# Weight quotients moved from VectorE to GpSimd in a cross-attention and block-quantised MLP kernel

## The chip, the cores and the metric

One core of a Trainium2 chip. The metric is device time of one launch in microseconds; less is better. PE is TensorE, DVE VectorE, ACT ScalarE, POOL (or Pool) GpSimd, SP SyncE, which here only issues DMAs.

## The reference

There are four batches (B = 4) of x [512, 512] and of a context [512, 256].

```python
x = x + x_att(layernorm(x), ctx)          # query = ctx Wq' + bq, key = ctx Wk' + bk
                                          # x_m = l . softmax(query key')'
x = x + ffn(layernorm(x))
# ffn: v = bf16(x); h = bf16(layernorm(v) * w + b)
#      h = bf16(mx(h) mx(W1)' + b1); h = bf16(gelu_tanh(h))
#      h = bf16(mx(h) mx(W2)' + b2); out = bf16(v + h)
def mx_quant(x):                          # blocks of 32 along the contraction axis
    amax = max(abs(block))
    scale = exp2(floor(log2(amax)) - 6)
    return clip(round(x / scale), -128, 127) * scale
```

W1 is [2048, 512] and W2 [512, 2048], both float32, and both are quantised on the chip in every launch.

## The kernel before, in words

Each engine has a program of its own, written out by hand in one order, and waits on semaphores; engines work strictly in that order. Batches are pipelined: while PE multiplies the attention of batch b, DVE and ACT prepare the softmax of batch b + 1 (its "front"), and ACT and Pool work on the second layernorm of batch b - 1.

**DVE** (from L760). `front(b, ...)` (L969) has, for each of four row tiles t, `negmax` (minus the row maxima of the energies in PSUM), `normalise` (x - mean, times the factor rx), `recip` and `recip_scaled` (one over the row sum, from ACT's exp), `p_low` and `x_low` (the low float16 halves of P and x). Between them stand the steps of the weights. A unit of weights is [128, 2048] float32; there are four of W1 and four of W2 (u = 0 to 3), and a unit takes seven steps, counted by `w_step`: `w_amax` (L791, largest of each block of 32), `w_power`, `w_scale`, `w_inverse` (tiny: power of two, scale and its inverse), `w_over` (L804, weight times inverse to int16), `w_clip` (L810), `w_mult` (L814, int16 times scale to bfloat16). `back(b, ...)` (L1032) holds `w_amax` of W2, the last `p_low`, the tail of an earlier batch (`times_w` and `plus_b` for four tiles: the layernorm's weight and bias into `hq`) and W1's clip and mult. `x_stats(b)` (L914) has four bn_stats and four bn_aggr of x for the next batch. `h1_*` is the same block quantisation for `hq`. The calls stand from L1057 on. After the batches come the slots (L1080), which quantise the gelu's output, 128 rows at a time.

**Pool** (from L335) has tiny operations on [128, 4]: `factors_x(b)` (from bn_aggr's output to `rx`; `normalise(b, 0)` waits for it), `mean_x1`, `factors_x1(b)` (scale and offset of the first normalisation of v; ACT's `v_out(b)` waits for `off`), `factors_v(b)` (from ACT's sums of v; `times_w(b, 0)` waits for it). Their order is set by `batch` and the calls from L410 on. In the MLP, Pool adds the residual, two operations of [128, 512] per tile.

**ACT** (from L436): `batch(b, front, qk, v)` (L511) has a loop over t with `exp`, `x_high`, `p_high`, `x_plus` (attention output of batch b from PSUM), `load_w1`/`load_w2` (DMA of the next unit, as soon as the one before has been read), `v_sums`, `v_out`, `context`; then `query_key` for the batch after and four `x1_square`. After the batches (L574 on): `v_out(2, .)`, `v_sums(2, .)`, then `x_plus(3, 0)`, `y_out(0, 0)`, and so on.

**PE** (from L610): `values(b, t)` (L652) waits for all four transposed tiles of P; `energies`, `queries_keys`. Its order in a batch (L667) is context, then `energies(front, t + 2)` and `values(b, t)` in turn, then the queries, keys and first two energies of the next. From L727: `values(3, 0)`, `product1(0, 0)`, `values(3, 1)`, `product1(0, 1)`, `values(3, 2)`, `values(3, 3)`, `product1(1, 0)`, and the steps of the MLP. `product1(m, k)` waits until `y_out` has read the PSUM banks of the tile before.

**SP** (from L214) issues the DMA transposes in order: four of x, four of P, then w2 of the unit before and w1 of this one, in each front (L231).

Of the kernel before, what the change touches and what calls it, by code (L numbers as in the profile page):

```python
# [15 lines left out]
P = 128  # L16
# [8 lines left out]
W_STEPS = 7  # L25
# [4 lines left out]
def xattn_ffn_kernel(nc, x, ctx_in, wq, bq, wk, bk, ln_w, ln_b, w1, b1, w2, b2, out):  # L30
# [25 lines left out]
    with ExitStack() as stack:  # L56
# [3 lines left out]
        def sem(name):  # L60
            return stack.enter_context(nc.semaphore(name))
# [106 lines left out]
        nm, off_rdy = sem("nm"), sem("off_rdy")  # L168
        v_mean, v_mean2, v_ms = sem("v_mean"), sem("v_mean2"), sem("v_ms")
# [166 lines left out]
        def _(pool):  # L336
# [49 lines left out]

            factors_x(0)
# [13 lines left out]
            def batch(b, x, v):  # L401

                if x is not None:
                    factors_x(x)
                if v is not None:
                    factors_v(v)
                mean_x1(b)
                factors_x1(b)
# [28 lines left out]
        def _(act):  # L437
# [73 lines left out]
            def batch(b, front, qk, v):  # L511

                for t in range(LT + 1):
                    if t < NT:
                        exp(front, t)
                        x_high(front, t)
                    if t > 0:
                        p_high(front, t - 1)  # L520
                    if b is not None and t > 1:
                        x_plus(b, t - 2)
                    if t == 2 and b is not None:
                        load_w2(front)
# [6 lines left out]
                if not isinstance(front, int) or front + 1 < B:  # L531
                    load_w1(front + 1)
# [229 lines left out]
        def _(dve):  # L762
# [41 lines left out]
            def w_over(a, u):  # L804
                dve.wait_ge(w_step[a], W_STEPS * u + 4)
                inverse = mxi[:, a, :, 0:1].broadcast_to([P, NB, BLOCK])
                dve.tensor_tensor(blocks(w_int[:, :]), blocks(wst[:, a, :]), inverse, ALU.mult)\  # L807
                   .then_inc(w_step[a], 1)

            def w_clip(a, u):  # L810
                dve.wait_ge(w_step[a], W_STEPS * u + 5)
                dve.tensor_scalar(w_int[:, :], w_int[:, :], QMAX, None, ALU.min).then_inc(w_step[a], 1)

            def w_mult(a, u):  # L814
                wait(dve, (w1T_rdy, w2T_rdy)[a], 16 * u)
                dve.wait_ge(w_step[a], W_STEPS * u + 6)
                dve.tensor_tensor(pairs(wquant[:, a, :]), pairs(w_int[:, :]), per_block(mxs[:, a, :, :]), ALU.mult)\
                   .then_inc(w_step[a], 1)
# [95 lines left out]
            def x_stats(b):  # L914
                if isinstance(b, int):
                    dve.wait_ge(ld_x[b], 16)
                for t in range(LT):
                    dve.bn_stats(stats[:, t, :], xs[:, LT * b + t, :]).then_inc(st, 1)  # L918
                if isinstance(b, int) and b > 0:
                    dve.wait_ge(rx_rdy, b)  # L920
                for t in range(LT):
# [47 lines left out]
            def front(b, w1, w2, stats_next, h1):  # L969

                negmax(b, 0)
                normalise(b, 0)
                if w1 is not None:
                    w_amax(W1, w1)

                negmax(b, 1)
                normalise(b, 1)  # L980
                recip(b, 0)
                if w1 is not None:
                    w_power(W1, w1)
                recip_scaled(b, 0)
                if w1 is not None:
                    w_scale(W1, w1)
                x_low(b, 0)
                if w1 is not None:
                    w_inverse(W1, w1)
                if h1 is not None:  # L990
                    h1_amax(h1)

                negmax(b, 2)
                normalise(b, 2)
                recip(b, 1)
                if h1 is not None:
                    h1_power(h1)
                recip_scaled(b, 1)
                p_low(b, 0)
                if h1 is not None:  # L1000
                    h1_scale(h1)
                x_low(b, 1)
                if h1 is not None:
                    h1_inverse(h1)
                if w2 is not None:
                    w_over(W2, w2)

                negmax(b, 3)
                normalise(b, 3)
                recip(b, 2)  # L1010
                if h1 is not None:
                    h1_over(h1)
# [3 lines left out]
                if h1 is not None:  # L1016
                    h1_clip(h1)
                if w2 is not None:
                    w_clip(W2, w2)
                    w_mult(W2, w2)  # L1020

                recip(b, 3)
                p_low(b, 2)
                recip_scaled(b, 3)
                x_low(b, 3)
                w_over(W1, b)
                if stats_next is not None:
                    x_stats(stats_next)
                if h1 is not None:
                    h1_mult(h1)  # L1030

            def back(b, w1, w2, tail):  # L1032


                w_amax(W2, w2)
                p_low(b, NT - 1)
                w_power(W2, w2)
                if tail is not None:
                    times_w(tail, 0)
                w_scale(W2, w2)  # L1040
                if tail is not None:
                    plus_b(tail, 0)
                w_inverse(W2, w2)
                if tail is not None:
                    for t in range(1, LT):
                        times_w(tail, t)
                        plus_b(tail, t)
                w_clip(W1, w1)
                w_mult(W1, w1)
# [15 lines left out]
            x_stats(0)  # L1065
            front(0, None, None, 1, None)
            back(0, 0, 0, None)
            front(1, 1, 0, 2, None)
            back(1, 1, 1, None)
            dve.wait_ge(ld_ln, 32)  # L1070
            front(2, 2, 1, 3, None)
            back(2, 2, 2, 0)
            for b in range(3, B):
                front(b, b, b - 1, None, b - 3)
                back(b, b, b, b - 2)
            for part in tail_parts(B - 3)[LT:]:
                for part_step in part:
                    part_step()
# [26 lines left out]
            w_over(W2, B - 1)  # L1105
# [50 lines left out]
```

## Time and profile before

| | us |
|---|---|
| median of 3 runs | 284.21 |
| lowest, highest | 283.39, 287.79 |
| profiled execution, its own time | 283.25 |
| its span in the profile | 281.4 |

| engine | busy us | share of the span |
|---|---|---|
| PE | 228.7 | 81% |
| DVE | 249.2 | 89% |
| ACT | 169.4 | 60% |
| POOL | 69.0 | 25% |

Times in the rows are microseconds from the start of the span. A timeline row has start, duration, engine, line, operation, output and input, and in brackets the idle time ahead of it and what ended that. In grouped rows the numbers behind the shapes are the count, the busy time with the mean of one in ns, and the idle time ahead of them. Consecutive instructions overlap by some 0.1 us, so that the distance of two starts is a little less than the duration. PEclk is TensorE's granted clock as a share of full speed.

### The profile page before, as it was taken

What the parts mean: (1) busy time and instruction counts of PE and PEld (TensorE: products, weight loads), DVE (VectorE), ACT (ScalarE), POOL (GpSimd) and SP (SyncE); (2) the same over time, 40 slices, a digit from 0 to 9 for tenths busy, and PEclk for the clock granted to TensorE, in tenths of its full rate; (3) what the DMA queues carried; (4) which work ended last, traced back from release to release, by engine and by line L of the source; (5) the groups of instructions that cost most, each with busy time, mean ns of one, the idle gap of its engine ahead of it and who ended that gap; (6) DMA issues with size and microseconds to landing.
All of it is one profiled execution on the core that took longest, in us unless ns stands there. A gap on an engine that the chain in (4) does not pass through costs nothing.

```text
span 281.4 us, 3244 instructions
## 1 busy us (share of the span) xinstructions
PE 228.7 (81%) x937; PEld 99.4 (35%) x946; DVE 249.2 (89%) x377; ACT 169.4 (60%) x287; POOL 69.0 (25%) x96
## 2 busy tenths in 40 slices
PE   7748739996998059651699969799999989999993
PEld 7314313443433024210244433344444434444431
DVE  2388999999988899999979999599999999877992
ACT  2337216628995447845987599966566554665610
POOL 1058100022004500053060050413333233333400
PEclk9985886999999759975899999999999999999999
DMA  4963999999997952939623045635355555555683
GB/s 157 378 250 89 227 279 201 297 238 194 263 257 190 221 91 38 222 59 194 124 52 62 0 93 70 119 62 123 88 122 129 130 130 131 130 130 114 139 178 130
DMA packets 103077, 42.92 MB, mean 152 GB/s; under 512 B 93844, under 2 KB 96152, under 8 KB 102552
## 3 DMA queue, kind: packets, MB, share of 16 engines
q1 hardware_dynamic: 100224, 35.93, 58.6%
q10 hardware_dynamic: 2360, 6.83, 7.7%
q8 instruction: 5, 0.08, 0.1%
q0 software_dynamic: 480, 0.02, 0.1%
q14 instruction: 8, 0.07, 0.1%
HBM read 15.48 MB, written 4.19 MB: 70 GB/s over the span
## 4 chain that ended last, share of the span: by engine, by line
DVE 45%; PE 25%; ACT 11%; DMA 8%; issue 5%; POOL 4%; SPq 2%; ACTq 0%; DVEq 0%; POOLq 0%
DVE amax L764 12%; PE ps L722 9%; PE ps L712 8%; PE ps L661 4%; DVE w_int L807 4%; DMA xhl<-pf 3%; DVE hq L966 3%; DVE stats L918 3%; DMA wst<-in_L_ffn_W 3%; DVE vw L961 3%; DVE pf L871 3%; DVE phl L942 2%; DVE wquant L861 2%; POOL rs L350 2%; DVE xhl L954 2%
## 5 line engine op out<-in xcount | busy, mean ns | idle before, releaser
L661 PE MATMUL ps<-pT,xT 128*128 128x512 f16 x192 | 49.7, 414 | 14.1 <-DMA pT<-phl 11.0
L722 PE MATMUL ps<-w2T,xhl 128*128 128x512 bf16 x247 | 56.5, 379 | 2.9 <-DMA xhl<-pf 2.4
L712 PE MATMUL ps<-w1T,cxT 128*128 128x512 bf16 x256 | 58.0, 380 | 0.0
L558 ACT ACTIVATE wst<-ps 128x1024 bf16<-128x1024 f32 x32 | 32.3, 1019 | 27.9 <-PE ps L712 27.9
L764 DVE TENSOR_REDUCE amax<-phl 128x64 f32<-128x2048 bf16 x16 | 36.5, 2280 | 6.9 <-ACT phl L562 6.9
L649 PE MATMUL ps<-qkT 128*128 128x512 f32 x32 | 19.5, 715 | 22.7 <-ACT pf L457 18.8
L661 PEld LDWEIGHTS ps<-pT,xT 128*128 128x128 f16 x192 | 19.9, 106 | 48.0 <-issue 31.8
L722 PEld LDWEIGHTS ps<-w2T,xhl 128*128 128x128 bf16 x256 | 24.6, 98 | 33.2 <-DMA xhl<-pf 4.2
L712 PEld LDWEIGHTS ps<-w1T,cxT 128*128 128x128 bf16 x256 | 23.7, 98 | 32.6 <-issue 6.2
L562 ACT ACTIVATE phl<-wst 128x2048 bf16<-128x2048 bf16 x16 | 30.6, 1910 | 1.3
L423 POOL TENSOR_TENSOR wst<-wst,vs 128x512 bf16<-128x512 bf16 x12 | 14.8, 1233 | 55.5 <-DVE wquant L866 55.5
L764 DVE TENSOR_REDUCE amax<-wst 128x64 f32<-128x2048 f32 x8 | 18.2, 2270 | 6.1 <-DMA wst<-in_L_ffn_W 6.1
L457 ACT ACTIVATE pf<-ps,nmax 128x512 f32<-128x512 f32 x16 | 10.9, 681 | 19.8 <-DVE nmax L928 19.7
L571 ACT ACTIVATE wst<-ps 128x512 bf16<-128x512 f32 x16 | 9.5, 595 | 16.2 <-PE ps L722 15.8
L861 DVE TENSOR_TENSOR wquant<-phl,mxi 128x2048 int16<-128x2048 bf16 x15 | 18.3, 1223 | 0.3
L641 PE MATMUL ps<-cxT,wqkT 128*128 128x512 f32 x32 | 16.5, 663 | 2.5 <-ACT cxT L447 2.5
L807 DVE TENSOR_TENSOR w_int<-wst,mxi 128x2048 int16<-128x2048 f32 x8 | 18.3, 2285 | 0.0
L871 DVE TENSOR_TENSOR pf<-wquant,mxs 128x2048 bf16<-128x2048 int16 x15 | 18.2, 1216 | 0.0
L649 PEld LDWEIGHTS ps<-qkT 128*128 128x128 f32 x32 | 5.9, 212 | 32.3 <-ACT pf L457 21.8
L355 POOL TENSOR_SCALAR rs<-mv 128x4 f32<-128x4 f32 x4 | 0.9, 227 | 65.6 <-DVE mv L923 65.6
L664 PE MATMUL ps<-xs,ident_x 128*128 128x512 f32 x32 | 16.3, 592 | 0.0
L482 ACT ACTIVATE xs<-ps 128x512 f32<-128x512 f32 x16 | 9.4, 586 | 9.7 <-PE ps L664 9.7
(79 smaller groups left out, 357.4 us busy)
## 6 DMA issues: line engine op xcount, KB each, us to landing
wst<-in_L_ffn_W ACTq DMA_DIRECT2D x6, 1024.0 KB, 6.1
xs<-in_x SPq DMA_DIRECT2D x4, 1024.0 KB, 8.4
out_x<-wst SPq DMA_DIRECT2D x16, 256.0 KB, 2.8
cx<-in_ctx SPq DMA_DIRECT2D x4, 512.0 KB, 5.8
wst<-in_L_ffn_W SPq DMA_DIRECT2D x2, 1024.0 KB, 10.3
xhl<-pf SPq DMA_TRANSPOSE x17, 4.3
xT<-xhl SPq DMA_TRANSPOSE x16, 4.6
pT<-phl SPq DMA_TRANSPOSE x16, 3.3
```

Of the source, the lines that this page charges most:

```text
L558: act.activation(ys[:, k, 1024 * g:1024 * g + 1024], ps_y[:, 2 * g:2 * g + 2, :], ACT.Copy)\
L562: act.activation(gs[:, k, :], ys[:, k, :], ACT.Gelu_apprx_tanh).then_inc(g_rdy, 1)
L641: last = pe.matmul(ps_qk[:, a, :], wqkT[:, a, c, :], cxT[:, c, :], start=(c == 0), stop=(c == CT - 1))
L649: pe.matmul(ps_e[:, t % 2, :], qkT[:, 0, P * t:P * t + P], qkT[:, 1, :], start=True, stop=True).then_inc(e_ps, 1)
L661: pe.matmul(ps_pv[:, t % 2, :], xT[:, t, NT * a + n, :], pT[:, :, NT * c + n, :], start=(s == 0), stop=False)
L664: pe.matmul(ps_pv[:, t % 2, :], ident_x[:, :], xs[:, LT * b + t, :], start=False, stop=True).then_inc(pv_ps, 1)
L712: last = pe.matmul(ps_y[:, c, :], h1T[:, k, t, :], w1T[:, 4 * c:4 * c + 4, t, :], start=False, stop=(t == KT - 1))
L722: last = pe.matmul(ps_z[:, k, :], h2T[:, k, t, :], w2T[:, t, :], start=False, stop=(t == FT - 1))
L764: dve.tensor_reduce(amax[:, a, :], by_block, AX_X, ALU.max, apply_absolute_value=True)\
L807: dve.tensor_tensor(blocks(w_int[:, :]), blocks(wst[:, a, :]), inverse, ALU.mult)\
L861: dve.tensor_tensor(pairs(h2u[:, k, :]), pairs(gs[:, k, :]), per_block(mxi[:, k, :, :]), ALU.mult).then_inc(h2_step[k], 1)
L871: dve.tensor_tensor(pairs(h2q[:, k, :]), pairs(h2u[:, k, :]), per_block(mxs[:, k, :, :]), ALU.mult).then_inc(h2_step[k], 1)
```

## The change

The quotient of each weight unit, `w_over` on DVE, becomes `over_scale` on Pool: in place in `wst`, in float32, counted by new semaphores `w_u`. `w_clip` on DVE reads `wst` and converts to int16, so a unit has six steps in place of seven. Pool's order is written out, with four waits (`p_lo` or `h_rdy`) ahead of W2's quotients. DVE's `front` has a new fixed order and takes in what `back` held. A unit of W2 gets its maxima in its own front and its clip and mult in the next. The tail of a batch stands between fronts, and `h1_*` behind `front(3)`, except `h1_amax(0)`. ACT's loop has one step more, and v's sums and outputs are one step later in it. In the diff, helpers and steps that only change place are left out.

```diff
-W_STEPS = 7
+W_STEPS = 6
...
+            def over_scale(a, u):
+                pool.wait_ge(w_step[a], W_STEPS * u + 4)
+                w = blocks(wst[:, a, :])
+                inverse = mxi[:, a, :, 0:1].broadcast_to([P, NB, BLOCK])
+                pool.tensor_tensor(w, w, inverse, ALU.mult).then_inc(w_u[a], 1)
+
+            over_scale(W1, 0)
             factors_x(0)
...
             factors_x(1)
-            batch(0, 2, None)
-            for b in range(1, B - 2):
-                batch(b, b + 2, b - 1)
-            batch(B - 2, None, B - 3)
-            factors_v(B - 2)
-            mean_x1(B - 1)
-            factors_x1(B - 1)
-            factors_v(B - 1)
+            pool.wait_ge(p_lo, NT)
+            over_scale(W2, 0)
+            over_scale(W1, 1)
+            factors_x(2)
+            mean_x1(0)
+            pool.wait_ge(p_lo, 2 * NT)
+            over_scale(W2, 1)
+            factors_x1(0)
+            over_scale(W1, 2)
+            factors_x(3)
+            factors_v(0)
+            mean_x1(1)
+            pool.wait_ge(h_rdy, LT)
+            over_scale(W2, 2)
+            factors_x1(1)
+            over_scale(W1, 3)
+            factors_v(1)
+            mean_x1(2)
+            pool.wait_ge(h_rdy, 2 * LT)
+            over_scale(W2, 3)
+            factors_x1(2)
+            factors_v(2)
+            mean_x1(3)
+            factors_x1(3)
+            factors_v(3)
...
-                for t in range(LT + 1):
+                for t in range(LT + 2):
                     if t < NT:
                         exp(front, t)
                         x_high(front, t)
-                    if t > 0:
+                    if 0 < t <= NT:
                         p_high(front, t - 1)
-                    if b is not None and t > 1:
+                    if b is not None and 1 < t < LT + 1:
                         x_plus(b, t - 2)
-                    if t == 2 and b is not None:
+                    if t == 1 and b is not None:
                         load_w2(front)
-                    if v is not None and t > 0:
-                        v_sums(v, t - 1)
-                    if v is not None and t < LT:
-                        v_out(v, t)
+                    if t == LT and front + 1 < B:
+                        load_w1(front + 1)
+                    if v is not None and t > 1:
+                        v_sums(v, t - 2)
+                    if v is not None and 0 < t <= LT:
+                        v_out(v, t - 1)
...
             def w_clip(a, u):
-                dve.wait_ge(w_step[a], W_STEPS * u + 5)
-                dve.tensor_scalar(w_int[:, :], w_int[:, :], QMAX, None, ALU.min).then_inc(w_step[a], 1)
+                wait(dve, w_step[1 - a], W_STEPS * (u + a))
+                dve.wait_ge(w_u[a], u + 1)
+                dve.tensor_scalar(w_int[:, :], wst[:, a, :], QMAX, None, ALU.min).then_inc(w_step[a], 1)
```

The new order of `front(b)` on DVE, in full ("later" is b > 0; `x_moments` and `x_aggregate` are the two halves of `x_stats`):

```python
negmax(b, 0)
w_amax(W1, b)                      # later
negmax(b, 1); normalise(b, 0); normalise(b, 1)
w_clip(W2, b - 1)                  # later
recip(b, 0); w_power(W1, b)        # later
recip_scaled(b, 0); w_scale(W1, b) # later
x_low(b, 0); w_inverse(W1, b)      # later
negmax(b, 2)
x_moments(b + 1)                   # b = 3: h1_amax(0)
recip(b, 1); normalise(b, 2); recip_scaled(b, 1); p_low(b, 0)
w_mult(W2, b - 1)                  # later
x_low(b, 1)
negmax(b, 3); w_clip(W1, b); recip(b, 2); normalise(b, 3)
recip_scaled(b, 2); p_low(b, 1); x_low(b, 2); w_mult(W1, b)
recip(b, 3); w_amax(W2, b); recip_scaled(b, 3); p_low(b, 2)
w_power(W2, b); x_low(b, 3); w_scale(W2, b)
x_aggregate(b + 1)                 # b < 3
w_inverse(W2, b); p_low(b, 3)
```

The calls: `x_moments(0)`, `x_aggregate(0)`, `front(0)`, `front(1)`, `front(2)`, `tail(0)`, `front(3)`, `h1_power` to `h1_mult` of batch 0, `tail(1)`, all six `h1_` steps of batch 1, then `w_clip(W2, 3)` and `w_mult(W2, 3)`, and from there as before. In W1's case `w_power` to `w_inverse` of unit 0 stand ahead of `x_moments(0)`, as before of `x_stats(0)`.

## Rows read from the trace of the kernel before

**Rows 1.** Windows: length, then busy PE, PEld, DVE, ACT, POOL; PEclk, DMA, GB/s.

```profile
39.00:65.60 26.60, 23.61 (x72) 9.82 (x73) 26.12 (x48) 14.37 (x32) 1.71 (x4) 0.87 1.11 248
65.60:100.10 34.50, 22.84 (x82) 9.75 (x79) 31.54 (x55) 24.41 (x59) 8.32 (x15) 0.92 0.97 215
100.10:134.40 34.30, 21.14 (x65) 8.46 (x66) 33.98 (x55) 22.89 (x55) 6.32 (x9) 0.75 0.62 124
```

**Rows 2.** Grouped instructions of 0 to 160 us: DVE's whole-unit and 512-wide operations.

```profile
L807 DVE TENSOR_TENSOR w_int<-wst,mxi 128x2048 int16<-128x2048 f32 x8 | 18.3, 2285 | 0.0
L764 DVE TENSOR_REDUCE amax<-wst 128x64 f32<-128x2048 f32 x8 | 18.2, 2270 | 6.1 <-DMA wst<-in_L_ffn_W 6.1
...
L928 DVE TENSOR_REDUCE nmax<-ps 128x1 f32<-128x512 f32 x16 | 10.9, 681 | 0.2 <-PE ps L649 0.2
...
L918 DVE BATCH_NORM_STATS2 stats<-xs 128x6 f32<-128x512 f32 x16 | 9.9, 680 | 0.0
...
L949 DVE TENSOR_SCALAR xn<-xs,mv,rx 128x512 f32<-128x512 f32 x16 | 8.6, 537 | 1.3 <-POOL rx L358 1.3
...
L812 DVE TENSOR_SCALAR w_int<-w_int 128x2048 int16<-128x2048 int16 x8 | 5.5, 687 | 0.0
```

**Rows 3.** The chain that ended last: first normalise, and the seam to batch 1.

```profile
18.90 0.56 DVE xn L949
...
36.69 3.09 SPq L244
39.83 3.21 DMA pT<-phl
```

**Rows 4.** Timeline of PE: values, queries and keys, first product.

```profile
43.28 4.51 PE L661 MATMUL ps<-pT,xT 128*128 128x512 f16 x12 [0.60 <-DMA pT<-phl]
...
59.69 3.60 PE L641 MATMUL ps<-cxT,wqkT 128*128 128x512 f32 x8
...
147.13 0.40 PE L707 MATMUL ps<-b1row,ones 3*128 3x512 bf16 x4
```

**Rows 5.** Timeline of all engines, 122 to 146 us.

```profile
124.76 5.36 SPq L244 DMA_TRANSPOSE pT<-phl  x4
...
131.79 0.75 DVE L966 SCALAR_TENSOR_TENSOR hq<-vw,rs,lnb 128x512 bf16<-128x512 f32 x1
...
132.64 2.93 ACT L497 ACTIVATE vs<-xs,off,rs 128x512 bf16<-128x512 f32 x4 [3.00 <-POOL off L370]
...
140.94 0.58 ACT L482 ACTIVATE xs<-ps 128x512 f32<-128x512 f32 x1
...
143.79 1.02 ACT L558 ACTIVATE wst<-ps 128x1024 bf16<-128x1024 f32 x1 [0.70 <-PE ps L712]
```

**Rows 6.** Timeline of POOL.

```profile
66.91 0.20 POOL L366 TENSOR_SCALAR rs<-sums 128x4 f32<-128x4 f32 x1 [4.53 <-ACT vs L490]
...
68.31 0.20 POOL L370 TENSOR_TENSOR off<-mean,rs 128x4 f32<-128x4 f32 x1
...
129.72 0.64 POOL L366 TENSOR_SCALAR rs<-sums 128x4 f32<-128x4 f32 x1 [3.04 <-ACT vs L490]
...
132.07 0.53 POOL L370 TENSOR_TENSOR off<-mean,rs 128x4 f32<-128x4 f32 x1
...
179.18 0.23 POOL L376 TENSOR_SCALAR mean<-sums 128x4 f32<-128x4 f32 x1 [12.82 <-ACT vs L508]
...
180.73 1.04 POOL L350 TENSOR_TENSOR rs<-rs,half 128x4 f32<-128x4 f32 x1
...
191.40 1.15 POOL L429 TENSOR_TENSOR wst<-xs,wst 128x512 f32<-128x512 f32 x1
```

**Rows 7.** Timeline of DVE: w_inverse and the power step of two units.

```profile
14.16 0.20 DVE L783 TENSOR_SCALAR mxi<-mxs 128x128 uint16<-128x128 uint16 x1
...
185.14 0.20 DVE L772 TENSOR_SCALAR pow<-amax 128x64 uint32<-128x64 uint32 x1
...
192.25 0.35 DVE L772 TENSOR_SCALAR pow<-amax 128x64 uint32<-128x64 uint32 x1
```

More of the change, by code:

```diff
@@ L912, in split3, with x_moments, x_aggregate @@
                 dve.tensor_copy(part[:, 2, :], f[:, 0, :]).then_inc(step, 1)
[L914 to L916 removed]
+            def x_moments(b):
+                dve.wait_ge(ld_x[b], 16)
                 for t in range(LT):
                     dve.bn_stats(stats[:, t, :], xs[:, LT * b + t, :]).then_inc(st, 1)
[L919 removed]
+            def x_aggregate(b):
+                if b > 0:
                     dve.wait_ge(rx_rdy, b)
+                    dve.wait_ge(xn_rdy, LT * b)
                 for t in range(LT):
@@ L967, in plus_b, with front @@
                                          ALU.mult, ALU.add).then_inc(h_rdy, 1)
-            def front(b, w1, w2, stats_next, h1):
+            def front(b):
+                later = b > 0
                 negmax(b, 0)
+                if later:
+                    w_amax(W1, b)
+                negmax(b, 1)
                 normalise(b, 0)
-                if w1 is not None:
-                    w_amax(W1, w1)
-                negmax(b, 1)
                 normalise(b, 1)
+                if later:
+                    w_clip(W2, b - 1)
                 recip(b, 0)
-                if w1 is not None:
-                    w_power(W1, w1)
+                if later:
+                    w_power(W1, b)
                 recip_scaled(b, 0)
-                if w1 is not None:
-                    w_scale(W1, w1)
+                if later:
+                    w_scale(W1, b)
                 x_low(b, 0)
[L988 to L991, printed above, removed]
+                if later:
+                    w_inverse(W1, b)
                 negmax(b, 2)
+                if b + 1 < B:
+                    x_moments(b + 1)
+                else:
+                    h1_amax(b - 3)
+                recip(b, 1)
                 normalise(b, 2)
-                recip(b, 1)
-                if h1 is not None:
-                    h1_power(h1)
                 recip_scaled(b, 1)
                 p_low(b, 0)
-                if h1 is not None:
-                    h1_scale(h1)
+                if later:
+                    w_mult(W2, b - 1)
                 x_low(b, 1)
[L1003 to L1006, printed above, removed]
                 negmax(b, 3)
+                w_clip(W1, b)
+                recip(b, 2)
                 normalise(b, 3)
-                recip(b, 2)
-                if h1 is not None:
-                    h1_over(h1)
                 recip_scaled(b, 2)
@@ L1015, in front, with tail @@
                 x_low(b, 2)
[L1016 to L1020, printed above, removed]
+                w_mult(W1, b)
                 recip(b, 3)
+                w_amax(W2, b)
+                recip_scaled(b, 3)
                 p_low(b, 2)
-                recip_scaled(b, 3)
+                w_power(W2, b)
                 x_low(b, 3)
[L1026 to L1049, printed above, removed]
+                w_scale(W2, b)
+                if b + 1 < B:
+                    x_aggregate(b + 1)
+                w_inverse(W2, b)
+                p_low(b, 3)
+            def tail(b):
+                for t in range(LT):
+                    times_w(b, t)
+                    plus_b(b, t)
             def tail_parts(b):
@@ L1064, in _ @@
             w_inverse(W1, 0)
[L1065 to L1069, printed above, removed]
-            dve.wait_ge(ld_ln, 32)
[L1071 to L1078, printed above, removed]
+            x_moments(0)
+            x_aggregate(0)
+            front(0)
+            front(1)
+            dve.wait_ge(ld_ln, 32)
+            front(2)
+            tail(0)
+            front(3)
+            h1_power(0)
+            h1_scale(0)
+            h1_inverse(0)
+            h1_over(0)
+            h1_clip(0)
+            h1_mult(0)
+            tail(1)
+            h1_amax(1)
+            h1_power(1)
+            h1_scale(1)
+            h1_inverse(1)
+            h1_over(1)
+            h1_clip(1)
+            h1_mult(1)
             def slot(m, k, tail, first=False, last=False):
```

18 lines of the change are left out of this document (2 added, 16 removed).

## Prediction, made before the changed kernel was run

> **What bounds the kernel now.** I read the busy table by stretches first, then the grouped instructions, then the chain that ended last, and last the timelines of the four engines around the seams between batches. The stretches [rows 1] are cut where DVE begins `front(1)` to `front(3)`: 39.0, 65.6 and 100.1 us. DVE is busy 26.1 of 26.6 us in batch 1, 31.5 of 34.5 in batch 2 and 34.0 of 34.3 in batch 3, so it looks like the bound, and eight `w_over` of 2.285 us are its dearest removable piece [rows 2]. But PE is busy 23.6 of 26.6 us in batch 1, and ACT 24.4 of 34.5 us in batch 2. So I looked at who stands just behind DVE.
>
> Seam 1 to 2: the last transposed P of batch 0 lands at 43.0 us [rows 3], PE begins `values(0,0)` at 43.3 and `queries_keys(2)` at 59.7 [rows 4], and DVE's `negmax(2,0)`, which needs the energies made from them, starts at 65.6 [rows 1]. DVE was just about on time: PE's path from landed P to the next energies is 65.6 - 43.3 = 22.3 us long.
>
> Seam to the MLP: `plus_b(1,3)` is over at 132.5, the offset `off` of batch 2 at 132.6, and ACT starts `v_out(2,.)` at 132.6, then the v sums, and reaches `x_plus(3,0)` at 140.9, the first half of `y_out(0,0)` behind it [rows 5]. PE begins `product1(0,1)` at 147.1 [rows 4]; it wants both halves of `y_out(0,0)`.
>
> **What is removed and added on DVE.** Eight `w_over` go: seven inside the batches, each holding the next instruction back by 2.2 us, one after them. `w_clip` now reads float32, not int16. Its price lies between 0.69 us (the int16 clip, L812) and 2.15 us (four times the 512-wide float32 tensor_scalar of L949, 0.537 us, start cost and all) [rows 2]. I take 1.4, nearer to L949 with the start cost paid once, 0.7 more than now. So batch 1, once 26.5 us of solid DVE work, would be 26.5 - 2 x 2.2 + 2 x 0.7 = 23.5; I use 22.5 to 23.5 for one `front`.
>
> **The quotient on Pool.** No Pool operation of 2048 columns is in the trace. Four times the 512-wide two-input one is 4.6 us [rows 6]; with start cost taken out (L370, 128x4, 0.2 us) it is 0.2 + 4 x 0.95 = 4.0. I take 4.3. A broadcast operand in blocks of 32 could make it dearer; 2.3 us (DVE's own time for it) and 9 us (double the 512 row's rate) are the far ends.
> The Trainium skill ("GPSIMD Engine Reference", section "Elementwise — side-by-side cycle accounting") has Pool's float32 tensor_tensor of 2048 at 4497 ns against 2293 on DVE; the trace agrees for DVE (2285 ns), and no row has the other. By it each quotient would be 0.2 us longer than I take.
>
> **Its gates.** A Pool operation under way holds DVE up. At 192.25 DVE's `power` takes 0.35 us while a Pool addition that ends at 192.55 is running; at 185.14, with Pool idle, it takes 0.20 [rows 6, 7]. The reductions that stand beside such additions keep their 2.28 us, like those without (the `w_amax`, 2.27 us [rows 2]).
> The Trainium skill ("SBUF — State Buffer", section "Who interferes with whom") says the same as a lock held for the whole instruction, against DVE operations in a two-port mode or with two SBUF inputs.
> So each quotient has a window. W2's: `negmax`, `w_amax`, `negmax` = 0.6 + 2.2 + 0.6 = 3.4 us, then `normalise`. W1's: `negmax` and four bn_stats = 0.6 + 2.4 = 3.0 us, then `normalise` [rows 2]. A quotient of 4.3 us leaves DVE waiting 4.3 - 3.4 = 0.9 us and 4.3 + 0.1 - 3.0 = 1.4 us: per batch 2.3 us of the 2 x (2.2 - 0.7) = 3.0 us saved are given back. From both sides the wait is 0 (no blocking) to 5 us each (9 us quotient).
>
> **Front(0).** `over_scale(W1,0)` is queued on Pool ahead of `factors_x(0)`. The first `normalise`, at 18.9 us [rows 3], needs that. The quotient starts near 14.4 us (as `w_inverse` ends [rows 7], beside the bn_stats) and ends near 18.7, and factors_x takes 1.7: normalise starts at 20.5, 1.6 us late. DVE then saves its 2.2 and pays 0.7. ACT comes to `query_key(1)` only after `p_high(0,3)`, which the new order has later. I get front(1) at 38.1, not 39.0.
> `p_low(0,3)` is now last in the front, at 37.2 (before 36.0, released at 36.7 [rows 3]), and, more important, `x_low(0,3)` is near 36 and SP transposes in order: xT 3, pT 0, 1, 2, 3. At a free queue four take 5.36 us [rows 5], 1.3 each: pT 3 is issued at 36.0 + 4 x 1.3 = 41.2 and lands 3.2 later, at 44.4. Beside a weight load one waits 3.09 us for its turn [rows 3]; with two such steps it is 48. W1(1) is loaded from 35.4 in the new order, so I take 45.0 against 43.0.
>
> **Batch 1 and 2.** PE's path is the later one: front(2) = 45.0 + 22.3 - 0.3 = 67.0 (DVE alone would be there at 38.1 + 23.2 + 1.4 = 62.7 and waits 4.3 us). That is 1.4 us later than before, although DVE does less. In front(2) ACT's v sums are one step later in its loop than before: `p_high(2,3)` is released by `recip_scaled(2,3)`, some 19.8 us into the front (22.5 less three 512-wide operations and small ones), plus 1.4 of lock. Then `p_high` 0.6, `x_plus` 0.7, load 0.4, v_sums 1.4, v_out 0.7, v_sums 1.4 (eight steps of v_out and v_sums took 140.9 - 132.6 = 8.3 us [rows 5]): 26.4. Pool's `factors_v` takes 2.6 (179.18 to 181.77 [rows 6]) and tail(0) 6.0, as before. Front(3) = 67.0 + 26.4 + 2.6 + 6.0 = 102.0, before 100.1.
>
> **Front(3) and what follows.** Here both locks count (W2's is let go by tail(0) itself): v sums end at 102.0 + 25.0 + 2.3 = 129.3; factors_v 131.9; tail(1), behind `h1_mult(0)`, which is over by then, ends at 137.9. Before, it ended at 132.5 [rows 5].
> Now the term that decides. Pool waits for `h_rdy` = 8 (the end of tail(1)), does `over_scale(W2,3)`, 4.3 us, and only then `factors_x1(2)`, 1.6 us alone (66.91 to 68.51) or 2.9 beside DVE's work (129.72 to 132.60) [rows 6]; I take 2.3. `off` is there at 137.9 + 4.3 + 2.3 + 0.2 = 144.7, before at 132.6. ACT is in order, so v_out(2), v_sums(2), `x_plus(3,0)` and `y_out(0,0)` all move by 12.1 us. PE had slack there: `y_out(0,0)` could have let product1(0,1) go at 140.94 + 0.7 + 2 x 1.0 = 143.6 and it started at 147.1 [rows 4, 5], because values(3,1) was in between, which is now done early: 3.5 us. Net 12.1 - 3.5 = +8.6.
> What is won beside that isn't waited for: product1(0,0) waits for the transposed W1(3), no longer a matter of the last DVE operation of the batch, and could start at 136, not 139.8; the last `w_over`, 140.6 to 142.8, has nobody waiting. From `product1(0,1)` on, nothing is changed, and PE, ACT and DVE keep their order, so the 8.6 us arrive at the end.
>
> **The sum.** The profiled execution took 283.25 us (span 281.4); 283.25 + 8.6 = 291.9. The median of the runs is 1.0 above it: 284.2 + 8.6 = 292.8.
> Ends. Low: no blocking (front(3) and tail(1) 2.3 + 1.4 earlier), landing at 44.4 (0.6), quotient 4.0 and factors 1.6 (1.0), tail stretches half a us shorter each: 8.6 - 6.3 = +2.3, so 286.5. High: landing at 48 (3.0), quotient 4.6 with its waits (1.2), factors 2.9 (0.6), and PE idle for over 10 us before product1(0,1), which in stretches where it idles so has a granted clock of 0.75 to 0.87 [rows 1], 1 us: +14, 298.
>
> **Rivals.**
> A, faster: the queues of ACT and Pool follow DVE instead of limiting it. For it: DVE's 91 to 99% in the three stretches [rows 1]. Seven times 2.2 - 0.7 = 10.5 us saved in the first stage; the part that can pass the join is the 4 us of product1(0,0) at least: 273.7 to 280, say 278. It needs `off(2)` before 136 us, and I find tail(1) alone ending later than that; against it also PE's 22.3 us path.
> B, within 2%: the same chain, with Pool and DVE not blocking each other and the transposes prompt: 286.5. For it: nothing in the trace shows a float32 DVE operation of 512 columns blocked.
> C, slower still: the broadcast quotient costs some 9 us. Then +4.7 directly at W2(3) and 4.7 in each of three locks and in front(0) that pass through: 284.2 + 8.6 + 4.7 + 10 = 307. Nothing for it but that no row shows such an operation.
> D, the change doesn't do what it says: a quotient stands beside reductions only for its first 3 us. That is part of my forecast.
>
> **How the numbers follow.** Forecast (288.5 to 297) 0.62, B 0.20, A 0.12, C 0.06. The likeliest is 292.8. The range, 285.5 to 298.5, takes in B and leaves out A and C and little more. Some 2% (5.7 us, above 289.9 or under 278.5) is what a measurement of this kernel can tell from no change: 0.58 of the forecast's 0.62 and C are over it; its other 0.04, B and 0.02 of A within. Slower 0.64, same 0.26, faster 0.10.
>
> **What would show it.** Right: Pool TENSOR_TENSOR of 128x2048 near 4.3 us; `normalise` lengthened right behind reductions; DVE idle some 4 us before `negmax(2,0)` and before tail(0); a Pool quotient between the last `plus_b` of tail(1) and `factors_x1(2)`, v_out(2) starting near 145; PE idle before product1(0,1) near 155. Wrong: front(3) starting before 95 us, or v_out(2) before 136; a span without those PE gaps.

## The result, and the profile after

The changed kernel takes 306.06 us (303.44 to 306.54, 4 runs) against 283.8 us: a ratio of 1.079, 95% interval 1.070 to 1.089. It is slower, as forecast, but by 22.3 us where 8.6 were forecast, and lies outside the range. A few executions of a kernel are over 1.5% slower than its fastest; medians here include them, ratios and intervals leave them out. The profiled execution took 306.54 us with a span of 304.7 us, 23.3 more than before.

The windows of the changed kernel, columns as in [rows 1], cut where DVE begins `front(1)`, `front(2)` and `front(3)`, where tail(1) ends, and at 205 us:

```profile
36.40:75.60 39.20, 24.20 (x81) 10.46 (x80) 22.32 (x44) 14.06 (x31) 13.25 (x9) 0.83 0.90 204
75.60:117.50 41.90, 25.10 (x82) 10.22 (x80) 27.98 (x52) 25.15 (x61) 9.87 (x14) 0.85 0.98 178
117.50:152.20 34.70, 21.10 (x69) 8.44 (x70) 32.11 (x52) 21.46 (x52) 12.37 (x11) 0.80 0.66 138
152.20:205.00 52.80, 42.73 (x190) 17.43 (x189) 42.61 (x51) 41.57 (x73) 12.03 (x19) 0.93 0.33 60
```

Front(1) begins at 36.4 us, 2.6 us earlier than before. Then batch 1 takes 39.2 us (before 26.6) and batch 2 takes 41.9 us (before 34.5), and DVE is busy for only 22.3 and 28.0 us of them, where it was busy for 26.1 and 31.5 [rows 1]. Batch 3 takes 34.7 us (before 34.3). So front(3) is 17.4 us late (117.5 against 100.1), and the other 23.3 - 17.4 = 5.9 us come after it.

What DVE and PE waited for, from their timelines (start us, us, instruction, idle before and releaser). DVE:

```profile
38.80 2.29 DVE L781 TENSOR_REDUCE amax<-wst 128x64 f32<-128x2048 f32 x1 [1.73 <-DMA wst<-in_L_ffn_W]
...
41.60 0.99 DVE L962 TENSOR_SCALAR xn<-xs,mv,rx 128x512 f32<-128x512 f32 x2
...
55.87 2.47 DVE L929 BATCH_NORM_STATS2 stats<-xs 128x6 f32<-128x512 f32 x4 [10.41 <-DMA xs<-in_x]
...
75.61 0.69 DVE L941 TENSOR_REDUCE nmax<-ps 128x1 f32<-128x512 f32 x1 [4.75 <-PE ps L666]
...
95.54 1.23 DVE L829 TENSOR_TENSOR wquant<-w_int,mxs 128x2048 bf16<-128x2048 int16 x1 [7.75 <-DMA w2T<-wquant]
```

PE:

```profile
53.28 4.82 PE L678 MATMUL ps<-pT,xT 128*128 128x512 f16 x12 [14.22 <-DMA pT<-phl]
...
168.76 0.61 PE L724 MATMUL ps<-b1row,ones 3*128 3x512 bf16 x4 [6.77 <-ACT wst L575]
169.31 5.71 PE L729 MATMUL ps<-w1T,cxT 128*128 128x512 bf16 x16
```

The three longest of these waits were not there before: DVE stands 10.41 us for the load of x(2), 7.75 us in `w_mult(W2,1)` for w2T(0), and PE 14.22 us for pT(0,3), which comes at 53.0 (before 43.0 [rows 3], when PE waited 0.60 us for it [rows 4]). All three are waits for DMAs. The timeline of the queues' issues shows what they ran beside. First ACT's issue of W2's load in batch 1, after and then before the change:

```profile
44.03 0.33 ACTq L494 DMA_DIRECT2D wst<-in_L_ffn_W  x1
```

```profile
49.38 0.33 ACTq L477 DMA_DIRECT2D wst<-in_L_ffn_W  x1
```

Then the issues of SP and ACT around w2T(0), in batch 2:

```profile
78.20 0.58 SPq L226 DMA_DIRECT2D xs<-in_x  x1
...
78.82 4.97 SPq L261 DMA_TRANSPOSE w2T<-wquant  x1
...
81.44 0.34 ACTq L494 DMA_DIRECT2D wst<-in_L_ffn_W  x1
...
83.84 11.37 SPq L255 DMA_TRANSPOSE w1T<-wquant  x1
```

And the chain of waits has how long the two transposes took to land:

```profile
43.72 9.32 DMA pT<-phl
...
53.28 4.82 PE ps L678 x12
...
75.61 0.69 DVE nmax L941
...
78.82 16.69 DMA w2T<-wquant
...
117.53 0.69 DVE nmax L941
...
152.28 3.64 POOL wst L393
...
157.82 2.93 ACT vs L514 x4
...
168.76 0.61 PE ps L724 x4
```

W2's load is issued at 44.03, right behind the transpose of pT(0,3) of 43.72, which then lands 9.32 us after its issue (before 3.2). In the kernel before that load was issued at 49.4. At 81.44 the next one goes out 2.6 us behind w2T(0), which takes 16.69 us. The last three rows are the join as forecast: tail(1) has ended, the quotient of W2(3) runs on Pool (152.28), the factors follow, ACT starts `v_out(2,.)` at 157.82 and PE `product1(0,1)` at 168.76. The wait of 6.77 us ahead of that has a second price. From 168.76 to 174.85 us TensorE's granted clock was 0.61, nearer to the lower of its two levels (half of full speed), and `product1(0,1)` took 6.1 us to the next `values`; before, after no such wait, the clock was 1.00 in that stretch and it took 3.8.

Pool's timeline, the first quotient and the join:

```profile
14.04 3.64 POOL L393 TENSOR_TENSOR wst<-wst,mxi 128x2048 f32<-128x2048 f32 x1 [11.78 <-DVE mxi L800]
...
152.28 3.64 POOL L393 TENSOR_TENSOR wst<-wst,mxi 128x2048 f32<-128x2048 f32 x1 [5.80 <-DVE hq L979]
156.01 0.28 POOL L367 TENSOR_SCALAR rs<-sums 128x4 f32<-128x4 f32 x1
156.37 1.04 POOL L351 TENSOR_TENSOR rs<-rs,half 128x4 f32<-128x4 f32 x1
157.49 0.30 POOL L371 TENSOR_TENSOR off<-mean,rs 128x4 f32<-128x4 f32 x1
```

The grouped instructions of 0 to 160 us:

```profile
L393 POOL TENSOR_TENSOR wst<-wst,mxi 128x2048 f32<-128x2048 f32 x8 | 29.1, 3641 | 31.7 <-DVE mxi L800 20.1 <-DVE hq L979 11.6
...
L824 DVE TENSOR_SCALAR w_int<-wst 128x2048 int16<-128x2048 f32 x8 | 9.7, 1216 | 0.0
...
L962 DVE TENSOR_SCALAR xn<-xs,mv,rx 128x512 f32<-128x512 f32 x16 | 9.1, 588 | 1.8 <-POOL rx L359 1.8
```

The quotient takes 3.64 us each time, the clip from float32 1.22 us, and `normalise` 0.59 us in the mean over sixteen (0.53 undisturbed): with the gates, the blocking that was priced at 2.3 us per batch is some 2 us in all (16 `normalise` 0.06 us longer each, and one `power` step, at 154.55, of 1.42 us where 0.19 is usual). In batches 1 and 2 DVE waited for x (10.41 and 1.23 us) while W1's quotient ran, so nothing was blocked there.

### The profile page after: what moved, and what is told of

Same layout as the page of the kernel before. It is cut to its first block, busy times and chain, and to the rows that moved or that the text cites. A ratio compares the mean times of both kernels' runs of the same rounds, so it can differ in the third digit from the quotient of the medians.

```text
span 304.7 us, 3264 instructions
## 1 busy us (share of the span) xinstructions
PE 231.5 (76%) x946; PEld 99.8 (33%) x946; DVE 237.6 (78%) x369; ACT 169.7 (56%) x287; POOL 92.6 (30%) x104
## 4 chain that ended last, share of the span: by engine, by line
DVE 32%; PE 25%; DMA 14%; ACT 13%; POOL 6%; issue 5%; SPq 4%; POOLq 0%; ACTq 0%; DVEq 0%
DVE amax L781 9%; PE ps L739 8%; PE ps L729 7%; PE ps L678 6%; DMA w2T<-wquant 5%; POOL wst L393 4%; DMA pT<-phl 3%; DMA xhl<-pf 3%; DVE vw L974 3%; DVE hq L979 3%; DMA wst<-in_L_ffn_W 3%; ACT squares L522 3%; SPq L245 2%; DVE pf L883 2%; ACT vs L514 2%
## 5 line engine op out<-in xcount | busy, mean ns | idle before, releaser
L678 PE MATMUL ps<-pT,xT 128*128 128x512 f16 x192 | 50.7, 420 | 37.4 <-DMA pT<-phl 25.8
L729 PE MATMUL ps<-w1T,cxT 128*128 128x512 bf16 x256 | 60.1, 389 | 0.0
L739 PE MATMUL ps<-w2T,xhl 128*128 128x512 bf16 x256 | 57.9, 379 | 1.2 <-DMA xhl<-pf 1.2
L393 POOL TENSOR_TENSOR wst<-wst,mxi 128x2048 f32<-128x2048 f32 x8 | 29.1, 3641 | 31.7 <-DVE mxi L800 20.1
L666 PE MATMUL ps<-qkT 128*128 128x512 f32 x32 | 18.5, 684 | 15.4 <-ACT pf L474 10.3
L486 ACT ACTIVATE xhl<-xn 128x512 f16<-128x512 f32 x16 | 10.0, 627 | 33.9 <-DVE xn L962 33.9
L974 DVE SCALAR_TENSOR_TENSOR vw<-vs,mean,lnw 128x512 f32<-128x512 bf16 x16 | 11.9, 746 | 13.4 <-POOL rs L351 13.4
L929 DVE BATCH_NORM_STATS2 stats<-xs 128x6 f32<-128x512 f32 x16 | 9.9, 680 | 11.6 <-DMA xs<-in_x 11.6
L873 DVE TENSOR_TENSOR wquant<-phl,mxi 128x2048 int16<-128x2048 bf16 x15 | 18.3, 1223 | 0.3
L883 DVE TENSOR_TENSOR pf<-wquant,mxs 128x2048 bf16<-128x2048 int16 x15 | 18.3, 1218 | 0.1
L356 POOL TENSOR_SCALAR rs<-mv 128x4 f32<-128x4 f32 x4 | 2.4, 608 | 48.6 <-DVE mv L937 48.5
```

The costliest lines, as they stand in the source:

```text
L393: pool.tensor_tensor(w, w, inverse, ALU.mult).then_inc(w_u[a], 1)
L666: pe.matmul(ps_e[:, t % 2, :], qkT[:, 0, P * t:P * t + P], qkT[:, 1, :], start=True, stop=True).then_inc(e_ps, 1)
L678: pe.matmul(ps_pv[:, t % 2, :], xT[:, t, NT * a + n, :], pT[:, :, NT * c + n, :], start=(s == 0), stop=False)
L729: last = pe.matmul(ps_y[:, c, :], h1T[:, k, t, :], w1T[:, 4 * c:4 * c + 4, t, :], start=False, stop=(t == KT - 1))
L739: last = pe.matmul(ps_z[:, k, :], h2T[:, k, t, :], w2T[:, t, :], start=False, stop=(t == FT - 1))
L873: dve.tensor_tensor(pairs(h2u[:, k, :]), pairs(gs[:, k, :]), per_block(mxi[:, k, :, :]), ALU.mult).then_inc(h2_step[k], 1)
```

## The experiments

The kernel before took 283.38 us beside the first four kernels that stand here (its repetition apart), 283.47 beside the three edits together and those built on them, 283.98 beside the two with the quotients on DVE, and 284.06 beside the repetition and the pair of two edits. All ratios are to these.

**The loads of x(2) and x(3) at once.**
```diff
             load_x(1)
+            load_x(2)
+            load_x(3)
...
-            front(0, None, 2)
-            front(1, 3, 3)
+            front(0, None, None)
+            front(1, 3, None)
```


> SP issues the loads of x(2) and x(3) at the start instead of behind the transposes of P. Theory A (the statistics of the next x, moved up in the front, stand before their data has landed): the idle 10.4 us ahead of x_moments(2) and 1.2 ahead of x_moments(3) go, and the time falls by about 10 us, to 296. Theory B (the weight load of W2, now issued one loop step earlier on ACT, shares the DMA engines with the transposes and delays them): the idle time only moves to negmax(1,3), because PE's values(0,0) still waits for transposed P until about 50 us; the time falls by 1 to 3 us, to 303 to 305, and the 7.7 us ahead of w_mult(W2,1) stay.

298.41 us (296.78 to 299.15), ratio 1.055 [1.051, 1.060], 7.7 us below the changed kernel. The wait for x(2) is gone, but pT(0,3) still lands 9.0 us after its issue and PE stands 13.7 us for it; DVE now waits 8.19 us for PE's energies instead, and front(2) starts at 75.1, where it did. So the 10.41 us for x(2) had hidden behind PE. What is won is w2T(0): with x(3)'s load out of its way it lands 4.5 us after its issue, DVE doesn't wait for it, and front(3) starts at 108.4. Neither theory held in full: A was right on the waits for x but had 10 us, B was right on PE but had the wait for w2T(0) stay.

**W2's load one step later.**
```diff
-                    if t == 1 and b is not None:
+                    if t == 2 and b is not None:
                         load_w2(front)
```


> ACT issues load_w2 at t == 2 again, not t == 1; nothing else. Theory A: no change beyond 1 us, since x(2) is issued where it was. Theory B: P(0,3) lands within 3 to 4 us of its issue, as before the change (near 47, not 53 us), w2T(0) lands within 8 us of its issue, not 16.7, so that the 7.7 us ahead of w_mult(W2,1) go; the time falls by 7 us or more, to 299 or less.

293.93 us (293.22 to 294.27), ratio 1.039 [1.034, 1.044], 12.1 us below the changed kernel. The load is issued at 54.6, behind the transposes; pT(0,3) lands 3.3 us after its issue, as theory B had it, PE begins `values(0,0)` at 47.2 instead of 53.3, w2T(0) takes 7.2 us (7.8 before the change) and nobody waits for it, and even the wait for x(2) is halved (5.45 us). Front(2) starts at 70.2, front(3) at 104.8. The load beside the transposes is thus the larger part of the two.

**The factors ahead of the quotient at the join.**
```diff
             mean_x1(2)
+            factors_x1(2)
             pool.wait_ge(h_rdy, 2 * LT)
             over_scale(W2, 3)
-            factors_x1(2)
```


> On Pool factors_x1(2) stands ahead of the gate h_rdy = 8 and of over_scale(W2,3), not behind them. Theory C (the step named in the prediction: ACT's v_out(2) and all behind it wait for off(2), which stands in Pool's queue behind tail(1) and a quotient): off(2) is there near 151, not 157.8 us, product1(0,1) starts near 162 and not at 168.8, and the time falls by 6 to 7 us, to 299.5. Rival: DVE or PE would be as late anyway, and the time stays within 1 us of 306.

293.51 us in the middle of 290.29, 291.79, 295.24 and 302.84; they are too far apart for an interval. In the profile `off(2)` is done at 144.7 with the quotient behind it, and PE's wait before `product1(0,1)` falls from 6.77 to 0.74 us. From front(3) to the end of the span it takes 290.0 - 110.0 = 180.0 us, where the changed kernel takes 304.7 - 117.5 = 187.2. That is the expected 7 us; but front(3) itself began at 110.0 and the whole fell by some 12.5 us, not 7, though nothing ahead of front(3) was edited. So it was run again:

> The same edit as the earlier kernel with the factors ahead of the quotient at the join and nothing else, in more runs, since that one's four spread from 290.3 to 302.8 us and had no interval. If the join alone is worth 6 to 8 us, the median is 298 to 300. If it is 293 or less again, the edit also changes how late w2T(0) lands, or the landing differs from one execution to the next; then the profile shows front(3) starting before 113 us, 117.5 in the changed kernel.

294.36 us (290.07 to 297.88, 6 runs), ratio 1.029 [1.020, 1.037]. Front(2) at 78.3 (pT(0,3) took 11.57 us to land), front(3) at 112.3 (w2T(0) took 9.99 us, 16.69 in the profile of the changed kernel), and from front(3) on 180.1 us again. The price of the join is firm; how badly the DMAs of batches 1 and 2 collide differs by 5 to 7.5 us between kernels whose instructions are the same up to there. Why wasn't found.

**Before's order, only the quotients on Pool.** Each is issued as soon as its inverse is there, without a gate; loads, transposes and W2's units stay where they were.
```diff
-                w_over(W2, w2)
+                w_clip(W2, w2)
...
-                w_over(W1, b)
+                w_clip(W1, b)
...
+            over_scale(W2, 1)
+            over_scale(W1, 2)
+            factors_x(3)
```


> The kernel before with only the quotients moved to Pool (float32, in place; w_clip reads wst and stands where w_over stood); DVE's, ACT's and SP's orders are those of before, and Pool's quotients have no gates but their data. Theory O (the loss is one of the new order, not of the quotient on Pool): DVE has 1.1 us less work per unit, the time is under before's, 276 to 281 us. Rival L (Pool's quotients hold DVE up by the port, or DVE holds them up, for what they save): within 2 us of before's 284, or above it.

290.95 us (289.61 to 292.06), ratio 1.029 [1.022, 1.035]: slower than before, where the theory had it faster. DVE's timeline in it, front(0) to front(2):

```profile
17.96 3.96 DVE L956 TENSOR_SCALAR xn<-xs,mv,rx 128x512 f32<-128x512 f32 x1 [1.30 <-POOL rx L359]
...
22.45 0.53 DVE L956 TENSOR_SCALAR xn<-xs,mv,rx 128x512 f32<-128x512 f32 x1
...
40.34 3.26 DVE L956 TENSOR_SCALAR xn<-xs,mv,rx 128x512 f32<-128x512 f32 x1
...
46.32 0.53 DVE L956 TENSOR_SCALAR xn<-xs,mv,rx 128x512 f32<-128x512 f32 x1
...
48.49 3.49 DVE L956 TENSOR_SCALAR xn<-xs,mv,rx 128x512 f32<-128x512 f32 x1
```

and Pool's:

```profile
18.01 3.64 POOL L392 TENSOR_TENSOR wst<-wst,mxi 128x2048 f32<-128x2048 f32 x1
...
38.78 4.54 POOL L392 TENSOR_TENSOR wst<-wst,mxi 128x2048 f32<-128x2048 f32 x1 [1.73 <-DVE mxi L795]
48.06 3.64 POOL L392 TENSOR_TENSOR wst<-wst,mxi 128x2048 f32<-128x2048 f32 x1 [4.74 <-DVE mxi L795]
```

A `normalise` of 0.53 us takes 3.2 to 4.0 us when a quotient is under way (17.96 beside 18.01, 48.49 beside 48.06); six such, a seventh of 1.29 and one of `power` (1.32 us) make 19.5 us more than undisturbed. Saved were 8 x (2.2 - 0.53) = 13.4 us, 2.2 a quotient less 0.53 for the dearer clip (1.22 against 0.69). The difference, 6.1, is most of the 7.6 us that the kernel lost. In the changed kernel, with its gates and its order of DVE, the blocking was some 2 us. Which of the two does it wasn't tried apart: no kernel has gates in before's order.

**The three edits together, and two of them.**

> The three edits x_early, w2_late and q_late together. If the three losses are separate places (late x data, W2's load beside the transposes, off(2) in Pool's queue), front(3) starts near 102 us, as the prediction had it, off(2) comes some 18 us after the end of the v sums' chain as in q_late (q_late's span past the start of front(3) was 179.9 us), and the time is 102 + 180 + 1.8 = 284, level with the kernel before. If two of them are one loss seen twice, it stays at 288 or more.

284.34 us (282.58 to 285.25, 10 runs), ratio 1.006 [1.002, 1.010], as expected: of the 22 us all but 0.9 are accounted for. But it is level with the kernel before, not faster. Its rows answer to those of the changed kernel. The chain of waits:

```profile
43.10 3.49 DMA pT<-phl
...
69.31 0.69 DVE nmax L943
```

PE's timeline:

```profile
148.29 0.40 PE L726 MATMUL ps<-b1row,ones 3*128 3x512 bf16 x4 [1.52 <-ACT wst L577]
```

pT(0,3) lands 3.49 us after its issue, front(2) begins at 69.3, front(3) at 102.6 and PE waits 1.52 us before `product1(0,1)`.

> The changed kernel with SP's loads of x(2) and x(3) issued right after x(1)'s and W2's load one step later, but Pool's order at the join left as it is: W2(3)'s quotient of 3.64 us ahead of the factors of the second normalisation. It stands against the same kernel with Pool's order also mended, 284.3 us. If the queue at the join has a price of its own (7.3 us were saved from front(3) on when it alone was mended), this one takes 290 to 292 us, and product1(0,1) begins some 6 us after the 143 to 146 of the mended one. Rival: the join's price was only there because batches 1 and 2 had come late, and the two parts are not additive: 284 to 287 us.

294.25 us (291.61 to 295.48), ratio 1.039 [1.034, 1.045]. Its PE timeline at the same place:

```profile
153.27 0.62 PE L726 MATMUL ps<-b1row,ones 3*128 3x512 bf16 x4 [6.44 <-ACT wst L577]
```

The join costs as much when everything ahead of it is on time: front(3) at 102.0, then 187.8 us to the end, against 180.0; by the medians it is 9.9 us (294.25 against 284.34), and the time lies somewhat above the expected 290 to 292. Counted from front(3), PE starts `product1(0,1)` 5.5 us later, and the rest comes with the slower clock behind that wait (granted 0.56; 6.6 us to the next `values` against 3.8). The join's price is additive; the two DMA edits are not (x's loads bring 2.8 us in front(3) once W2's load is moved, and nothing that the medians show: 294.25 against 293.93).

**The v sums one step earlier**, beside the three edits.
```diff
-                    if v is not None and t > 1:
-                        v_sums(v, t - 2)
                     if v is not None and 0 < t <= LT:
-                        v_out(v, t - 1)
+                        v_sums(v, t - 1)
+                    if v is not None and t < LT:
+                        v_out(v, t)
```


> As x_w2_q, and ACT's v_sums and v_out one loop step earlier, where they were before the change. Theory V (DVE's idle time ahead of each tail, 4.8 us at tail(0), comes from v's sums being a step later): the idle time ahead of tail(0) and tail(1) falls by about 2 us each, and the time by 3 to 4 us, to 280 to 281. Rival: v_out a step earlier puts 1.5 us of ACT work ahead of exp and x_high, which delays p_high as much; no change.

283.35 us (281.71 to 284.44), ratio 1.000 [0.996, 1.004]: 1.0 us instead of 3 to 4, and hardly clear of the noise, since the two intervals overlap. DVE's idle time ahead of the tails falls from 8.8 to 6.9 us, but its wait for PE's energies grows from 9.0 to 10.5, and front(3) starts at 103.1.

**P's first two transposes ahead of x's last**, in SP's order, beside those four edits and in the kernel before.
```diff
-                for t in range(LT):
+                for t in range(LT - 1):
                     x_transpose(t)
+                p_transpose(0)
+                p_transpose(1)
+                x_transpose(LT - 1)
+                p_transpose(2)
+                p_transpose(3)
```


> As all4, and SP issues the transposes of P(0) and P(1) ahead of that of x(3). The new order of DVE makes the low half of x(3) last but four, so that all four transposes of P queue behind it at 1.3 us each. Theory S (that burst sits on the path from P to PE's values): values(0,0) starts 2 to 3 us earlier and the time falls by 2 to 3 us against all4. Rival: SP then waits for P(1) before it may issue x(3), or DVE is the later one by now: no change.

280.36 us (278.57 to 282.01, 10 runs), ratio 0.991 [0.985, 0.996]: 3.0 us, the fastest of all. PE begins `values(0,0)` at 45.0, front(2) is at 66.9 and front(3) at 99.3.

> The same edit of SP on the kernel before, whose DVE is busy throughout. Its P(0,3) is released last anyway and PE's path was level with DVE's at 65.6 us: no change beyond 1 us, 283 us. If it gains 2 us or more, PE's path and not DVE set the kernel before's time as well.

282.85 us (280.5 to 286.15), ratio 0.998 [0.993, 1.003]: nothing, as expected. DVE doesn't wait for PE at that seam in it, but pT(0,3) doesn't land earlier either (43.6 against 43.0), so it isn't a test of what an earlier one would bring.

**The quotients back on DVE**, float32 and in place, ahead of the clip, in the fastest order and in the changed kernel.
```diff
-                pool.tensor_tensor(w, w, inverse, ALU.mult).then_inc(w_u[a], 1)
...
+                dve.tensor_tensor(w, w, inverse, ALU.mult).then_inc(w_u[a], 1)
                 wait(dve, w_step[1 - a], W_STEPS * (u + a))
                 dve.wait_ge(w_u[a], u + 1)
```


> all4_pt with each quotient back on DVE, right ahead of its clip, still in float32 and in place; Pool has none. It prices the move itself where its collisions are gone. Theory M (the move is worth DVE's time less what DVE waits for PE, ACT and Pool anyway): DVE has 2.2 us more per quotient, of which all4_pt's idle time (6.4 us for PE, 6.9 for Pool's factors) hides a part; the time rises by 4 to 10 us, to 284 to 290. Rival: DVE is no bound in this order at all, and the time stays within 2 us of 280.

293.89 us (292.71 to 296.01), ratio 1.033 [1.024, 1.042]. The grouped instructions of it, then of the same order with the quotients on Pool:

```profile
L821 DVE TENSOR_TENSOR wst<-wst,mxi 128x2048 f32<-128x2048 f32 x8 | 18.3, 2285 | 0.0
```

```profile
L404 POOL TENSOR_TENSOR wst<-wst,mxi 128x2048 f32<-128x2048 f32 x8 | 29.1, 3641 | 27.2 <-DVE mxi L811 21.3 <-DVE hq L990 5.8
```

So the move to Pool is worth 13.5 us there, more than expected: 18.3 us of quotients leave DVE (its busy time falls by 15.1 us, 253.4 to 238.3, since some `normalise` are longer), and its waits for Pool, PE's energies and the weight loads are nearly the same with them there (6.9 + 5.3 + 8.2 = 20.4 us, with the quotients on Pool 6.9 + 6.4 + 7.7 = 21.0), so the waits hide next to nothing. Two things limit what the 13.5 us say. The clip still reads float32, which before's form on DVE did not: by 8 x 0.53 = 4.2 us (an estimate, from 1.22 and 0.69) they overstate the move. And against the kernel before this order with its quotients on DVE loses 9.9 us (293.89 against 283.98), so that all of it together, the fastest kernel here, gains 3.1 us (280.36 against 283.47).

> The changed kernel with each quotient back on DVE, right ahead of its clip; Pool has none, all else is the change's. Theory R (the 22 us are the new order's: late x, W2's load beside the transposes, v's sums a step later; not Pool's work): still far over before's 284, at 300 to 312: the waits for x(2), P(0,3) and w2T(0) stay, 3.6 us of quotient go from Pool's queue ahead of off(2), some 2.2 us per quotient are added on DVE and partly hidden. Rival: Pool's quotients are the loss, and it falls to 290 or less.

301.26 us (299.9 to 301.89), ratio 1.057 [1.049, 1.064]. With the quotients on DVE the changed order is still 17.3 us slower than before, of which the float32 clip can make 4.2. So most of the loss comes with the order, not with Pool's arithmetic. But the waits are not all the same, where the expectation had them stay: ACT's load of W2 goes out at 48.2, 3 us behind pT(0,3), PE begins `values(0,0)` at 48.9 and not at 53.3, w2T(0) takes 11.6 us, and DVE waits 3.6 us for x and 2.3 for w2T. How the 17.3 us divide wasn't worked out.

## Why the prediction was right in its direction and wrong in its size

The time from front(3) to the end of the span splits all of it into two parts:

| kernel | front(3) begins | from there to the end |
|---|---|---|
| before | 100.1 | 181.3 |
| forecast | 102.0 | 188.0 |
| after | 117.5 | 187.2 |
| x early | 108.4 | 186.6 |
| W2's load late | 104.8 | 186.6 |
| both | 102.0 | 187.8 |
| factors first, two profiles | 110.0, 112.3 | 180.0, 180.1 |
| all three | 102.6 | 180.0 |

- "Now the term that decides" was right in its mechanism. `off` of batch 2 was to come 42.7 us after front(3) began (144.7 - 102.0) and came after 40.3 (157.8 - 117.5); the quotient was 3.64 us, not 4.3. The stage after front(3) was to cost 6.7 us more than before, and cost 5.9. That these are so near is partly luck. `product1(0,1)` was to start 6.7 us later after front(3) than before, and started 4.2 later (51.2 us after it, before 47.0); another 1.7 us came behind it, where the forecast had nothing in its sum and 1 us at its high end: the low granted clock after PE's wait. Undoing that one order gives back 7.1 to 7.8 us there (187.2 against 180.0 and 180.1, 187.8 against 180.0).
- The step that failed is "Batch 1 and 2": front(2) = 67.0 and front(3) = 102.0, from a landing of pT(0,3) put at 45.0, with 48 as its high end. It landed at 53.0: it was issued 1.9 us later than that had it (43.7 against 45.0 - 3.2 = 41.8) and took 9.3 us in place of 3.2. So front(2) began at 75.6: 53.3 + 22.3, as that step had PE's path. Behind it, in front(2), DVE waited another 7.75 us for w2T(0), a wait that the sum put at nothing. The forecast looked at the order of SP's transposes, and at W1's load, but not at which DMAs other engines would now issue at that moment: ACT's load of W2 moved up 5.3 us onto pT(0,3) because ACT's step t = 1 comes earlier in the new order and, a batch later, together with SP's load of x(3), onto w2T(0). The load of x(2), which came too late for `x_moments(2)` in its new place, was not in the sum either, but cost nothing here, since PE was later. With both loads out of the way front(3) begins at 102.0 and 102.6, where the forecast had it, but by luck: front(2) begins at 68.8 and 69.3 and not at 67.0, and front(2) then takes 33.3 us and not 35.0. Of the late start 0.6 us is a slip in the sum (PE begins 0.3 us after the landing, so it is 45.0 + 22.3 + 0.3 = 67.6), the rest is mainly a landing at 46.9 and 46.6 in place of 45.0.
- "The quotient on Pool" and the clip: 3.64 us against 4.3 and 1.22 against 1.4. Both were taken too dear by small amounts. The Trainium skill ("GPSIMD Engine Reference", section "Elementwise — side-by-side cycle accounting") has 4497 ns for a float32 tensor_tensor add of this size; the trace has 3641 ns for this multiply, whose second operand is a broadcast bfloat16, and the measurement decides.
- "Its gates": the mechanism is shown by the kernel in before's order (3.2 to 4.0 us for an instruction of 0.53), and the Trainium skill's rule ("SBUF — State Buffer", section "Who interferes with whom") agrees with it. The size inside the gates was put at 2.3 us per batch; it was under 1 us, since the quotient was shorter and the windows held nearly all of it (in the kernel with all three edits, without the waits for x, `normalise(b,2)` takes 1.04, 1.04 and 1.22 us where 0.53 is undisturbed). Rival B, the same chain without the blocking, differed from the forecast by this.
- "Front(0)": 38.1 forecast, 36.4 measured. `normalise` did not start late by 1.6 us but by 0.6. ACT's `query_key(1)` behind `p_high(0,3)` is what front(1) waits for in the end, as that step had it, but for 0.6 us only. The landing of pT(0,3), which that step also gives, is the one that failed above.
- Rival A (the queues follow DVE) was wrong for this kernel, but not for the idea: with the loads, the join, v's sums and P's transposes reordered, moving the quotients brings 13.5 us within that order, though only 3.1 us against the kernel before. Rivals C and D are out: no quotient took over 4.62 us in any kernel, and they do stand where they were put. That rival C's 307 us is next to the measured 306.06 is chance.

## What to carry to other kernels

When a change moves steps in a loop, list for every DMA queue what each engine now issues at each seam, and look for big loads that come to lie within a few microseconds of the transposes that the next stage waits for; here that was worth more than the term that looked decisive (11.8 us by the medians and 15.5 in the profiles, against 9.9 and 7.8). Work moved to an engine with little to do still has a place in that engine's order: put it behind, not ahead of, the small operations that another engine waits for. A stage-by-stage subtraction (start of a stage, and from there to the end) shows which part of a forecast held, also when the total didn't.

## What the runs showed of the hardware that was not expected

- The transpose of pT(0,3) landed 3.2 to 3.6 us after its issue with no load on ACT's queue close behind it, 8.8 to 11.6 us with a 1 MB load issued there 0.3 to 0.8 us later. A 1 MB load of x on SP's own queue 1.4 us behind it left it at 3.2 and 3.3 us (the kernel before, and W2's load late).
- w2T(0) took 4.5 us without x(3)'s load ahead of it (W2's load 4.3 us behind), 7.2 to 7.8 us with x(3)'s load 0.6 us ahead and W2's 7.7 us or more behind, and 10.0 to 16.7 us with x(3)'s ahead and W2's 2.6 to 4.3 us behind. W2's loads took 8.4 (batch 1) and 14.2 us (batch 2) in the changed kernel, against a median of 5.5 us.
- After a wait of 6.8 us, PE's granted clock was 0.61 in the next 6.1 us, and `product1(0,1)` took all of them (6.6 us at 0.56 in the kernel with two of the edits, after 6.4 us); after waits of 0.7 to 1.5 us it took 3.8.
- Two kernels with the same instructions up to there differed by 7.5 us in when front(3) began (110.0 and 117.5); the cause stays open.
- Pool's float32 multiply of 128x2048 with an operand broadcast in blocks of 32 takes 3.64 us, and 4.54 and 4.62 us the two times that it began beside DVE's 2048-wide multiply; DVE's own takes 2.285 us. Each DVE `normalise` that came behind it waited until it had ended.
